# Attention stage of a macaron block: scores in pairs on the row halves of TensorE, the mask as matmuls, maxima by pairs, one bank for products

## The reference, cut to what matters

```
q = (x @ q_w + q_b) / sqrt(8);  k = x @ k_w + k_b;  v = x @ v_w + v_b    # x normalised, 16 heads of 8
scores = einsum("bhqd,bhkd->bhqk", q, k)                                  # 1024 x 1024 for each of 64 (b, h)
scores = where(causal, scores, finfo(float32).min)
attn = softmax(scores, axis=-1)
ctx = einsum("bhqk,bhkd->bhqd", attn, v)
```

## Time and profile before

| | |
|---|---|
| three runs, us | 2671.39, 2673.97, 2681.03 (median 2673.97) |
| profiled execution, own time | 2672.96 us |
| its span | 2671.2 us |
| busy in the span | PE 1847.3 us, PEld 1034.2, DVE 1659.7, ACT 949.1, POOL 944.6 |
| costliest group | masked reduction, line 733, 1536 times, 823.9 us, mean 582 ns |
| granted TensorE clock | mean 0.839 of full |

### The profile page before, as it was taken

The page is one execution under the profiler, slowest core; times in us unless marked ns, Lnnn a source line. Parts: engine busy times, 40 slices in busy tenths (PEclk is TensorE's granted clock), DMA queues, the critical chain, the costliest instruction groups (busy, mean ns, idle before and its releaser), DMA issues. The chain is left out here.

```text
span 2671.2 us, 45728 instructions
## 1 busy us (share of the span) xinstructions
PE 1847.3 (69%) x10834; PEld 1034.2 (39%) x10928; DVE 1659.7 (62%) x5110; ACT 949.1 (36%) x1988; POOL 944.6 (35%) x1548
## 2 busy tenths in 40 slices
PE   3499889899710981499990075479998899840693
PEld 2133333333510770289980043223333333330472
DVE  7488778787350224867764485688887788451223
ACT  2256556566400330100000032336665566510231
POOL 4022222222445440068770563012222222337342
PEclk8689999999755995689995588679999999855797
DMA  3501111110002435000003001301011110001344
GB/s 84 212 14 26 27 27 26 25 24 6 1 25 68 124 113 146 0 0 0 0 4 36 16 16 47 106 25 26 26 25 27 27 26 14 1 4 51 109 135 128
DMA packets 109183, 120.08 MB, mean 45 GB/s; under 512 B 31264, under 2 KB 71584, under 8 KB 107936
## 3 DMA queue, kind: packets, MB, share of 16 engines
q1 hardware_dynamic: 92448, 96.50, 13.8%
q0 software_dynamic: 8192, 16.86, 1.9%
q10 hardware_dynamic: 8320, 4.19, 0.6%
HBM read 71.01 MB, written 45.71 MB: 44 GB/s over the span
## 5 line engine op out<-in xcount | busy, mean ns | idle before, releaser
L733 DVE CUSTOM_DVE_ANT_0 pA<-pA,causal 128x512 f32<-128x512 f32 (+3 forms) x1536 | 823.9, 582 | 183.0 <-PE pA L576 172.7
L777 ACT ACTIVATE wt<-pB 128x512 f32<-128x512 f32 (+3 forms) x1536 | 654.3, 496 | 442.2 <-PE pB L617 290.2
L818 POOL TENSOR_SCALAR_AFFINE_SELECT wt<-wt 128x128 f32<-128x128 f32 x1024 | 290.7, 293 | 767.6 <-ACT wt L777 746.3
L576 PE MATMUL pA<-ka,qa 125*128 125x512 bf16 (+3 forms) x1536 | 486.7, 343 | 71.1 <-PEq L272 30.0
L617 PE MATMUL pB<-qa,ka 128*128 128x512 bf16 (+3 forms) x1442 | 428.6, 333 | 51.9 <-issue 23.8
L633 PE MATMUL pC<-wt,va 128*32 128x512 f32 (+3 forms) x3072 | 347.5, 499 | 0.0
L617 PEld LDWEIGHTS pB<-qa,ka 128*128 128x128 bf16 x1536 | 145.2, 97 | 420.5 <-ACT wt L777 256.9
L576 PEld LDWEIGHTS pA<-ka,qa 125*128 125x128 bf16 x1536 | 147.5, 98 | 248.7 <-DVE mx L733 164.5
L733 DVE DVE_READ_ACCUMULATOR2_ANT mx<- 128x1 f32 x1536 | 217.0, 141 | 0.0
L1209 POOL DMA_INDIRECT y<-eo,dest x128 | 122.5, 957 | 185.3 <-issue 112.4
L1071 POOL DMA_INDIRECT xin<-keep_v,keep_send x128 | 126.9, 992 | 82.6 <-DVE keep_send L1044 43.8
(11 more groups left out here) (236 smaller groups left out, 2430.5 us busy)
## 6 DMA issues: line engine op xcount, KB each, us to landing
w<-in_L_ffn_fc_w_dram SPq DMA_DIRECT2D x64, 256.0 KB, 2.8
qa<-qk_parts SPq DMA_DIRECT2D x192, 64.0 KB
ka<-qk_parts SPq DMA_DIRECT2D x192, 64.0 KB
xi<-xin SPq DMA_DIRECT2D x32, 258.0 KB, 3.6
qk_parts<-qp SPq DMA_DIRECT2D x24, 256.0 KB, 2.4
qk_parts<-kp SPq DMA_DIRECT2D x24, 256.0 KB, 2.8
xin<-zero SPq DMA_DIRECT2D x4, 1032.0 KB, 7.1
y<-zero SPq DMA_DIRECT2D x4, 1024.0 KB, 13.1
```

The lines of the kernel that those rows point to most:

```text
L576: pe.matmul(slot(s, n)[:, 0:b - a], qa[s.stage][0:MROW, h, i * P:(i + 1) * P], ka[s.stage][0:MROW, h, a:b], start=True, stop=True).then_in ...
L733: vec.tensor_tensor_reduce(out=slot(s, n)[:, 0:size], in0=slot(s, n)[:, 0:size], in1=mask, scale=1.0, scalar=LOWEST, op0=ALU.add, op1=ALU.max,
L777: act.activation(wt[g % NW][h][:, 0:e - a], pB[(g * GH + h) % NB][:, 0:e - a], ACT.Exp).then_inc(exp_done, 1)
L818: pool.affine_select(out=block_, in_=block_, compare_op=ALU.is_ge, fill=0.0, base=0, pattern=[[1, P]], channel_multiplier=-1).then_inc(mas ...
```

## The change

Scores and pieces work on pairs of heads. Head 2p uses partitions 0 to 63 and head 2p+1 partitions 64 to 127 of the q and k buffers, and each matmul addresses only 48 (pieces) or 51 rows (scores) from 0 or from 64. The buffers are half as wide. Each of the 12 loads becomes two.

```
-            sp.dma_start(dst[r * HD:(r + 1) * HD, :, :],
-                         w["qk_parts"][which, split[r], bass.ds(u, 1)]
-                         .rearrange("o (h d) t -> (o d) h t", d=HD)).then_inc(a["qk_loaded"][stage], 16)
+            for side in range(2):
+                at = side * HROW + r * HD
+                sp.dma_start(dst[at:at + HD, :, :],
+                             w["qk_parts"][which, split[r], bass.ds(u, 1)]
+                             .rearrange("o (p s d) t -> s (o d) p t", s=2, d=HD)[side]).then_inc(a["qk_loaded"][stage], 16)
```

```
+                    diagonal = b == (i + 1) * P
+                    out = slot(s, n)
+                    for q in range(2):
+                        rows = side(q, KROWS)
+                        last = pe.matmul(out[:, q, 0:b - a], qa[s.stage][rows, p, i * P:(i + 1) * P],
+                                         ka[s.stage][rows, p, a:b], start=True, stop=not diagonal)
+                    if diagonal:
+                        for part, skip in (("lo", 0), ("hi", HROW)):
+                            for q in range(2):
+                                rows = side(q, HROW)
+                                last = pe.matmul(out[:, q, b - a - P + skip:b - a], c["pick_" + part][rows, :],
+                                                 c["future_" + part][rows, skip:], start=False, stop=part == "hi")
+                    last.then_inc(a_done, 1)
...
-                            vec.tensor_tensor_reduce(out=slot(s, n)[:, 0:size], in0=slot(s, n)[:, 0:size], in1=mask,
-                                                     scale=1.0, scalar=LOWEST, op0=ALU.add, op1=ALU.max,
-                                                     accum_out=mx[a // HALF][:, i, h:h + 1]).then_inc(a_used, 1)
+                            vec.reduce_max(mx[a // HALF][:, i, 2 * p:2 * p + 2], slot(s, n)[:, :, 0:b - a],
+                                           AX).then_inc(a_used, 1)
+                            if e == LATE:
+                                late = slice(HT, BT)
+                                vec.wait_ge(a_used, event(s, n))
+                                vec.tensor_tensor(top[:, late, :], mx[0][:, late, :], mx[1][:, late, :],
+                                                  ALU.max).then_inc(top_ready, 1)
```

```
-                    reached(pe, exp_done, v.u * NCH + (g * GH + h - (NB - 1)))
-                    pe.matmul(pB[(g * GH + h) % NB][:, 0:e - a], ka[v.stage][0:P, h, j * P:(j + 1) * P],
-                              qa[v.stage][0:P, h, a:e], start=True, stop=True).then_inc(st_done, 1)
+                    reached(pe, exp_done, v.u * NCH + (g * GH + 2 * p + 1 - (NB - 1)))
+                    for h in (2 * p, 2 * p + 1):
+                        rows = side(h, KROWS + 3)
+                        pe.matmul(pB[(g * GH + h) % NB][:, 0:e - a], ka[v.stage][rows, p, j * P:(j + 1) * P],
+                                  qa[v.stage][rows, p, a:e], start=True, stop=True).then_inc(st_done, 1)
...
+                        done = GROUP[g - LAG]
+                        for p in range(PAIRS):
+                            scores(s, g, p)
+                            passed += (e - a) / PAIRS + ((done[2] - done[1]) * LEAD if p == PAIRS - 1 else 0)
...
                         if g >= LAG:
-                            products(s, g - LAG)
-                            passed += behind * (1 - LEAD)
+                            products(s.shift(-1), g - LAG)
+                        elif not fixed(s, 1):
+                            products(s.shift(-2), NG + g - LAG)
+                        passed += (done[2] - done[1]) * (1 - LEAD)
...
+                def copy_low(s):
+                    act.wait_ge(pv_done, s.u * NCH - NCH)
+                    if not fixed(s, 2):
+                        act.wait_ge(a_done, before(s) - (NEV - ORDER[2].index(CTX_LO) - 1))
+                    copy_context(0)
```

More of the change, by code:

```diff
@@ L516, in ffn_attention, with side @@
                                                         sem("pv_done"), sem("cT_ready"))
-        dve = sem("dve_a")
+        dve, split_link = sem("dve_a"), sem("split_link")
+        top_ready = sem("top_ready")
+        def side(h, rows):
+            return slice((h % 2) * HROW, (h % 2) * HROW + rows)
         def fixed(s, upto):
@@ L654, in step @@
                         if g >= LAG:
-                            products(s, g - LAG)
-                            passed += behind * (1 - LEAD)
-                    for g in range(NG - LAG, NG):
-                        passed += GROUP[g][2] - GROUP[g][1]
-                        while n < count and sum(share[:n + 1]) <= sum(share) * passed / total:
-                            run(s, n)
-                            n += 1
-                        products(s, g)
+                            products(s.shift(-1), g - LAG)
+                        elif not fixed(s, 1):
+                            products(s.shift(-2), NG + g - LAG)
+                        passed += (done[2] - done[1]) * (1 - LEAD)
+                    while n < count:
+                        run(s, n)
+                        n += 1
                 def last_b(s):
                     step(s, len(FINAL))
+                    for g in range(NG - LAG, NG):
+                        products(s.shift(-1), g)
                     for n in range(len(FINAL), len(order(s))):
@@ L752, in last @@
+                            if e == LATE:
[3 more added lines that the diff above has]
+                                                  ALU.max).then_inc(top_ready, 1)
                 def last(s):
-                    vec.wait_ge(a_used, before(s))
-                    for k in range(4):
-                        split(s, 0, k, k)
@@ L806, in stage, with split, split_high, split_low @@
                                      .rearrange("p (t h r) -> p t h r", t=BT, h=GH)).then_inc(v_staged[s.stage], 1)
+                def split(s, half, links):
+                    t = slice(half * HT, (half + 1) * HT)
+                    src = top if half else mx[0]
+                    parts = [mparts[:, t, :, r] for r in range(3)]
+                    pool.tensor_copy(parts[0], src[:, t, :]).then_inc(split_link, 1)
+                    apart(pool, split_link, links + 1)
+                    pool.tensor_tensor(rest[:, t, :], src[:, t, :], parts[0], ALU.subtract).then_inc(split_link, 1)
+                    apart(pool, split_link, links + 2)
+                    pool.tensor_copy(parts[1], rest[:, t, :]).then_inc(split_link, 1)
+                    apart(pool, split_link, links + 3)
+                    pool.tensor_tensor(parts[2], rest[:, t, :], parts[1], ALU.subtract).then_inc(mparts_ready, 1)
+                def split_high(s):
+                    apart(pool, top_ready, s.u + 1)
+                    split(s, 1, s.u * (LINKS_LO + LINKS_HI))
+                def split_low(s):
+                    apart(pool, a_used, before(s))
+                    split(s, 0, s.u * (LINKS_LO + LINKS_HI) - LINKS_LO)
                 def first(s):
@@ L810, in first, with step @@
                         stage(s.shift(d))
-                def mask(s):
+                    split_high(s)
+                def step(s, more=True):
                     v = s.shift(-1)
@@ L819, in mask @@
                                                pattern=[[1, P]], channel_multiplier=-1).then_inc(masked, 1)
-                def step(s):
-                    mask(s)
-                    if not isinstance(s.u, int) or s.u + 2 < UNITS:
-                        apart(pool, pv_done, s.u * NCH)
-                        stage(s.shift(2))
-                attention_steps(pool, step, mask, first)
+                        if g == SPLIT_LO:
+                            split_low(s)
+                        if g == SPLIT_HI and more:
+                            split_high(s)
+                    if more and not fixed(s, 1) and (not isinstance(s.u, int) or s.u + 1 < UNITS):
+                        apart(pool, pv_done, s.u * NCH - NCH)
+                        stage(s.shift(1))
+                attention_steps(pool, step, lambda s: step(s, False), first)
 def ffn_output(core, keep, w, c, tag):
```

155 lines of the change are left out of this document (61 added, 94 removed).

## The result

The changed kernel takes 2789.8 us (median of four, 2789.2 to 2804.9), the kernel before beside it 2674.1: a ratio of 1.0442, interval 1.0402 to 1.0483. It is slower by 116 us where the forecast had 37. The sign and the wide range held, the forecast's own range (to 2774) did not. The profiled spans are 2788.7 and 2671.2 us.

What follows compares the result with a forecast made beforehand. A chain through PE, ACT and DVE was taken to bound the units; 11 x (+1.6) + 4 x (-0.4) + 3 gave +19 a stage, +38 for both, 2673 to 2711 us; likeliest case 2654 to 2774, wide range 2570 to 2840.

Steps and rivals of the forecast that it cites:

- 11 ordinary units: Attention units without a loop turn, per stage: 35.4 us each instead of 33.8, so +1.6 each.
- turns: Units holding a loop turn, four a stage: about 37.2 us against 37.6, so -0.4 each.
- The clock falls: Rival for the attention units: granted clock of 0.9 makes work cost 2.7 us more, 2792 us; chance 0.12.
- The walk: Step-by-step timing of one attention unit: 35.4 us, three slow places; units of 33.5 to 37.5 given chance 0.48.
- (c): Unit's end: TensorE ready at 33.5 us, the high maxima's rows arrive through DMAs at 35.45.
- group 8: Four pieces behind one another with two slots; the fourth waits for VectorE's second reduction, 4.8 us for the group.
- (a): Group 2: ScalarE's copy after the previous unit's products delays the first exponential 0.45 us; second pair at 6.9.
- Row halves don't overlap: Rival: a 512-column pair costs its two matmuls in sequence, 0.44 us; unit 39.4, total 2831 us; chance 0.10.
- The saved work shows: Rival: waits shrink with VectorE's work; unit 28 us, total 2489, or 2600 with half; chance 0.30.
- Part 2: Pieces in pairs with the mask on TensorE: masks taken at 0.2 us per diagonal piece, 3.2 us a unit.
- Part 4: One product bank: ScalarE's low-half copy waits for the previous unit's last products, now after group 1's scores.
- Part 5: Outside the units: projection loads double from 36 to 72 at half size; +3 us a stage, bounds 0 to +12.

Runs made afterwards that it cites:

- e3: Changed kernel with the high maxima's transposes two pieces earlier in TensorE's order; 2697.9 us, ratio 1.008.
- h3: Changed kernel with idle matmul pairs in TensorE's waits: six ahead of the first score pair, two ahead of six second pairs; 2742.5 us, ratio 1.026.
- f4: Kernel before with plain maxima over unmasked scores in place of VectorE's masked reductions; 2643.7 us, ratio 0.988.
- e4: Changed kernel without the four mask matmuls of each diagonal piece; 2846.4 us, ratio 1.063.
- f1: Changed kernel with the products of a unit's last two groups put back behind that unit's last scores; 2864.4 us, ratio 1.070.
- h1: Changed kernel with at most two pieces between two score pairs; 2768.8 us, ratio 1.035.
- h4: Changed kernel with the high maxima one piece earlier in TensorE's order; 2730.6 us, ratio 1.020.
- e1: Changed kernel with every piece's pair of matmuls issued twice into the same place; 2860.7 us, ratio 1.068.
- h2: Changed kernel with GpSimd's six memsets of the query and key buffers made twice in each projection; 2801.1 us, ratio 1.047.

## Why the prediction was wrong

The sum by its terms, first stage (units between copies of the high maxima; three intervals hold a turn, not four):

| term | forecast, us | measured |
|---|---|---|
| 11 ordinary units | +17.6 | +46.7 (37.7 each, for 33.5) |
| turns | -1.6 | +12.3 (41.8 each, for 37.7) |
| first and last unit | 0 | +11.7 (first interval 4.5, end 7.1) |
| projection | +3 | -2.5 |

**The failed step is in the sum: units at 35.4 us, 24 us of work and 11.5 of waits, priced at a grant of 1.00.** "The clock falls" stood among the rivals with 0.12 and 2792 us (measured 2789.8), its sign to look for "ordinary units under 0.95" (0.86). The walk itself was right: at a grant of 1.00 the unit is 34.8 (e3 and the wait) to 35.0 us (h3), its three slow places at their places, (c) with 1.43 for 1.95 us, group 8 with 4.6 for 4.8, and (a) in h3's unit at full clock with group 2 at 5.3 us and its second pair at 6.7, for 5.4 and 6.9:

```profile
438.92 0.38 PE L654 MATMUL pB<-qa,ka 51*128 51x512 bf16 x2
...
444.26 0.39 PE L654 MATMUL pB<-qa,ka 51*128 51x512 bf16 x2
...
445.59 0.39 PE L654 MATMUL pB<-qa,ka 51*128 51x512 bf16 x2 [0.50 <-ACT wt L789]
```

The clock adds 2.7 to 2.9 us to an ordinary unit, (37.7 - 34.9) x 22 = 62 us in both stages, and it is also what the two other terms missed: behind a turn's stop come some 13 us at half clock, so that the fetch doesn't "cover (c)" for nothing (41.8 for 37.2), and the last unit, without pieces, runs at a grant of 0.71 where it had 1.00.

Why 0.12 was too little can be read before the change: in the earlier trace rows a turn showed 0.95 where its neighbours showed 1.00. Behind its stop come 3.4 us at half clock (the profile of the kernel before, TensorE and a window):

```profile
282.20 0.63 PE L617 MATMUL pB<-qa,ka 128*128 128x512 bf16 x1 [3.54 <-issue]
...
282.20:285.60 3.40, 3.27 (x12) 1.24 (x11) 1.31 (x7) 2.76 (x7) 0.33 (x2) 0.50 0.52 122
```

In five of the six turns of both stages a stop sets off a fall even in the dense kernel. The walk then wrote down 11.5 us of waits in 35, one of 2 us just where a unit's first scores wait for each other, and the forecast did not put the two together. The rival's number was right by luck: it spreads 0.9 evenly and adds 2.7 us in each of 30 intervals (81 us), where the falls lie at the boundary and add 62 us in the 22 ordinary units, the rest at turns and in the first and last units. Some of the forecast's small sums are off without consequence: 52.08 + 72 x 0.34 is 76.6 and not 76.9, and 24 and 11.5 make 35.5.

**Row halves don't overlap** is refuted (0.22 us a pair). **The saved work shows**: f4 shows how little VectorE's part gives, 0.8 us a unit for half of it. The rival's own point, waits under 6 us, wasn't reached. Part 2's masks were overpriced in work and, by e4, earn their place through the clock. Part 4 (a) stands, but the same shift of the products is worth 75 us (f1). Part 5's +3 had the wrong sign; ScalarE's wait for the stores stayed at 12.0 us (12.2 before), and what changed in the first projection was a cost the forecast had not looked at: VectorE beside the memsets.

The Trainium skill, "TensorEngine Tiling (Array Packing)", Key Properties, has the array drained at a change of tiling mode; by it 0.6 us a unit had been set against the walk. The trace is in line with the rule and gives a smaller price. A context block comes 0.32 us behind the start of a 512-column score pair (0.21 of streaming at 2.4 GHz), where before, with both at full height, it was 0.22:

```profile
358.66 0.38 PE L617 MATMUL pB<-qa,ka 128*128 128x512 bf16 x1
358.88 0.38 PE L596 MATMUL pA<-ident,cT 128*128 128x128 f32 x2
...
503.43 0.39 PE L645 MATMUL pB<-qa,ka 51*128 51x512 bf16 x2 [0.49 <-ACT wt L776]
503.75 1.09 PE L622 MATMUL pA<-ident,cT 128*128 128x128 f32 x8
```

That is 0.1 us a block. The block of the maxima starts 0.10 us behind the streaming of what it follows in both kernels, so the change adds nothing there, and ahead of the two context blocks it adds 0.2 us a unit. The unit came out under the walk all the same, since the masks had been priced some 0.1 us each too high, 16 times a unit.

Open: the 5.5 us of the second projection; and the stretch between the stages varies by 10 us over versions of the changed kernel that don't touch it (1053 to 1063 us from the last context to the next first maximum), so that its 10.9 us less in the changed kernel is not fully a gain. h1's and h4's gains were not divided into clock and wait. h3's ordinary units are at full clock, but its turns take 40.1 to 43.8 us, about as long as the changed kernel's, filler included.

## What to carry to other kernels

Thinning out TensorE's work can slow a kernel that waits: a walk of a stage has to say for every wait what the engine does before and after it, and price the 3 to 13 us behind it at half clock where a stop or a run of waits stands among thin work (3.4, 10.2 and 13.7 us were seen here). A sign that could have been read in this case is a stage of the old kernel whose grant falls at its loop turns. A transfer on the path is to be issued with room to spare: moving one block of transposes by two pieces was worth 92 us. Filler matmuls in the waits are a quick test for such a loss (beside other work they only cost), and leaving work out is another.

## What the runs showed of the hardware

- Leaving out a quarter of TensorE's instructions (276 to 212 a unit) made the kernel 57 us slower, at a grant of 0.69 for 0.81 in the stage.
- The grant falls behind waits far shorter than a full stop: 0.81 us busy in 488 to 491 us and the fall at 491.7, with single waits of 1.43 and 0.76 us; in e3 behind two waits on VectorE of 0.47 and 0.81. It came back after 3.4 us there, after 10.2 in the changed kernel, after 13.7 at a turn.
- The same 9216 columns of idle pairs a unit won 47 us in TensorE's waits (h3) and cost 71 us beside the pieces (e1).
- Four mask matmuls behind a 512-column piece cost under 0.1 us at full clock, weight loads and all.
- Going from a 512-column score pair on row halves to a full-height transpose took 0.32 us from start to start, from a full-height score 0.22.
- VectorE's fp32 normalisation of 128 columns takes 0.34 us alone. Beside GpSimd's memsets it lasts as long as they do: 3.4 to 3.6 us beside those of 3.65 (kernel before), 1.7 to 1.9 beside those of 1.94 (h2). The Trainium skill, "SBUF — State Buffer", "SBUF: two separate sides", describes a port pair that one of the two engines takes for a whole instruction while the other is blocked; the trace agrees, and shows more than one instruction of waiting: in the changed kernel the first two normalisations lasted 5.9 and 5.7 us, until the last of five memsets in a row was done.
